# Reordering the last 90 microseconds of a fused cross-attention and expert-scaled feed-forward kernel

## What is computed

```python
def xattn(hs, ctx, mask, bias, ln_w, w_q, w_k, w_v, w_out):     # 32 heads of 128
    q, k, v = rmsnorm(hs, ln_w) @ w_q.T, ctx @ w_k.T, ctx @ w_v.T
    p = softmax(where(mask, q @ k.T + bias, -inf)); p = where(mask, p, 0)
    return hs + (p @ v) @ w_out.T

def ffn(x, weight, bias, gate_w, in_scale, out_scale):          # 8 experts, soft routing
    routing = softmax(x @ gate_w.T)
    return (x * (routing @ in_scale)) @ sign(weight).T * (routing @ out_scale) + bias

x = x + xattn(layernorm(x), ...)
x = x + ffn(layernorm(x), ...)
```

## Time and profile before

| what | us |
| --- | --- |
| median of 3 runs | 860.38 (859.5 to 860.78) |
| the profiled execution | 857.39 |
| its span, first to last instruction | 855.6 |
| PE / DVE / ACT / POOL busy | 840.8 / 630.6 / 390.4 / 301.8 |
| mean granted PE clock | 0.990 |

### The profile page before, as it was taken

The page is one execution under the profiler, slowest core; times in us unless marked ns, Lnnn a source line. Parts: engine busy times, 40 slices in busy tenths (PEclk is TensorE's granted clock), DMA queues, the critical chain, the costliest instruction groups (busy, mean ns, idle before and its releaser), DMA issues.

```text
span 855.6 us, 12845 instructions
## 1 busy us (share of the span) xinstructions
PE 840.8 (98%) x4348; PEld 705.3 (82%) x4348; DVE 630.6 (74%) x1011; ACT 390.4 (46%) x1005; POOL 301.8 (35%) x279
## 2 busy tenths in 40 slices
PE   9999999999999999999999999999999999999897
PEld 8878888888888877888888888888888888888775
DVE  5777846878775886867777777777787777789755
ACT  5633412432432444545554455455445545556642
POOL 2103211022020144534644544554354455423236
PEclk9999999999999999999999999999999999999969
DMA  8354464673453768314214412431442143150002
GB/s 278 127 194 170 158 218 135 208 241 123 136 173 106 233 197 285 123 53 151 105 53 154 151 67 91 152 111 52 149 152 88 69 153 112 47 209 7 1 0 100
DMA packets 60576, 114.07 MB, mean 133 GB/s; under 512 B 5192, under 2 KB 38600, under 8 KB 55264
## 3 DMA queue, kind: packets, MB, share of 16 engines
q1 hardware_dynamic: 60512, 113.25, 38.8%
HBM read 77.58 MB, written 35.65 MB: 132 GB/s over the span
## 4 chain that ended last, share of the span: by engine, by line
PE 87%; DVE 7%; issue 2%; ACT 2%; DMA 1%; POOL 0%; DVEq 0%; POOLq 0%; ACTq 0%; SPq 0%
PE out L1241 10%; PE out L1243 10%; PE out L1242 10%; PE proj L1241 8%; PE proj L1243 8%; PE proj L1242 8%; PE s L1313 6%; PE o L1332 6%; PE s L1243 3%; PE s L1241 3%; PE s L1242 3%; PE t L1321 3%; PE t L1360 1%; PE proj L1399 1%; PE s L1289 1%
## 5 line engine op out<-in xcount | busy, mean ns | idle before, releaser
L848 ACT ACTIVATE probs<-probs,neg_max 128x128 f32<-128x128 f32 x256 | 99.7, 391 | 137.3 <-DVE neg_max L1099 137.2
L697 POOL TENSOR_TENSOR w_stage<-w_stage 128x256 f32<-128x256 f32 x30 | 25.0, 833 | 309.1 <-DMA w_stage<-in_wk 132.7
L709 POOL TENSOR_TENSOR w_lo<-w_stage,w_hi 128x512 fp32r<-128x512 f32 (+1 forms) x52 | 59.2, 1149 | 144.8 <-ACT w_hi L786 144.8
L1131 DVE TENSOR_TENSOR acc<-out,acc 128x512 f32<-128x512 f32 x112 | 76.2, 687 | 36.5 <-PE out L1243 35.8
L1241 PE MATMUL out<-wo_hi,o_hi 128*128 128x512 f32 x224 | 95.1, 425 | 0.6 <-DVE acc L1131 0.6
L1241 PE MATMUL proj<-x_hi,w_hi 128*128 128x512 f32 x210 | 88.5, 422 | 0.2 <-DVE ring L958 0.2
L1243 PE MATMUL out<-wo_lo,o_hi 128*128 128x512 f32 x224 | 88.2, 394 | 0.0
L1242 PE MATMUL out<-wo_hi,o_lo 128*128 128x512 f32 x224 | 87.6, 391 | 0.0
L1243 PE MATMUL proj<-x_lo,w_hi 128*128 128x512 f32 x210 | 82.7, 394 | 0.0
L1242 PE MATMUL proj<-x_hi,w_lo 128*128 128x512 f32 x210 | 82.0, 391 | 0.0
L719 POOL TENSOR_TENSOR bias_mask<-bias_raw,mask_neg 128x512 f32<-128x512 f32 x64 | 76.0, 1199 | 14.5 <-DVE probs L1096 14.5
(11 more groups left out here) (318 smaller groups left out, 2153.3 us busy)
## 6 DMA issues: line engine op xcount, KB each, us to landing
k_spill<-ring SPq DMA_DIRECT2D x64, 256.0 KB, 2.7
v_spill<-ring SPq DMA_DIRECT2D x64, 256.0 KB, 2.2
w_stage<-in_wk SPq DMA_DIRECT2D x32, 256.0 KB, 3.4
big_stage<-in_wv SPq DMA_DIRECT2D x8, 1024.0 KB, 7.9
w_stage<-in_wq SPq DMA_DIRECT2D x32, 256.0 KB, 4.2
k_first<-k_spill SPq DMA_DIRECT2D x8, 1024.0 KB, 6.8
v_first<-v_spill SPq DMA_DIRECT2D x8, 1024.0 KB, 4.8
wo_raw<-in_wo SPq DMA_DIRECT2D x16, 512.0 KB, 3.3
```

Source lines behind the costliest of these rows:

```text
L709: pool.tensor_tensor(lo, staged(m, part), hi.bitcast(F32), ALU.subtract).then_inc(g_wlo, 1)
L848: last = act.activation(probs[:, j % 2, b, :], probs[:, j % 2, b, :], ACT.Exp, bias=neg_max[:, col:col + 1], accum_out=row_sum[:, col:col ...
L1131: dve.tensor_tensor(acc[:, b, :], out_bank[n % 2][:], acc[:, b, :], ALU.add).then_inc(v_acc, 1)
```

## The change

- The output products of the last two pairs, b and c, of one tile go into the same bank: c adds to what b left there. Tiles 0 to 7 use `proj0, proj1, out0, out1, out0, out1, proj0, proj1`. DVE adds only once for both.
- The steps of the last eight units are set anew: `ST` and the adds are spread differently, and `b`'s last tiles, `TX 0` and `TX 1` stand inside the last slot.
- `SCALES` goes from slot j + 4 to j + 2, and its low part from DVE to POOL, between two `BM`.
- `TX` uses the two score banks for all tiles.
- Tiles 4 and 6 are normalised by DVE, 5 and 7 by ACT. ACT's square root has a step of its own, `ROOT`.
- POOL's bias additions are steps of their own, `BI`, and several of them stand much later.
- `M` is cut into two parts (chunks 0 and 1, chunks 2 and 3), and the order of the feed-forward steps is new: tiles 0 and 1 are routed and multiplied before tiles 4 to 7 are transposed.
- A new step `KEEP` issues six matmuls of 512 columns whose result nobody reads.

```diff
@@ schedule()
-    steps += swift(j + 2, outs(a, 7), outs(b, 0), [("SIGN", 2)])
+    steps += swift(j + 2, outs(a, 7), outs(b, 0), [("SIGN", 2), ("SCALES",)])
     steps += swift(j + 3, outs(b, 1), outs(b, 2), [("SIGN", 3)])
-    steps += swift(j + 4, outs(b, 3), outs(c, 0), [*outs(c, 1), ("SCALES",), *outs(c, 2)])
-    steps += swift(j + 5, [], [("ST", 0), ("ST", 1), ("ST", 2), *outs(c, 3)], [])
-    steps += swift(j + 6, [], [("ST", 3), ("LN2", 0), *outs(b, 4)], [("LS", 0)])
-    steps += swift(j + 7, outs(b, 5), [("NT", 0), ("NT", 1), *outs(b, 6)], [("NT", 2), ("NT", 3)])
-    steps += [*outs(b, 7), ("TX", 0), ("TX", 1), *outs(c, 4), ("ST", 4), ("TX", 2), ("TX", 3), *outs(c, 5), ("ST", 5), ("G", 0),
-              *outs(c, 6), ("ST", 6), ("ROUTE", 0), *outs(c, 7), ("ST", 7), ("RT", 0), ("RTC", 0), ("LN2", 1), ("G", 1), ("R", 0),
-              ("LS", 1), ("NT", 4), ("NT", 5), ("NT", 6), ("NT", 7), ("TX", 4), ("TX", 5), ("OS", 0), ("TX", 6), ("TX", 7), ("OS", 1),
-              ("ROUTE", 1), ("Y", 0), ("G", 2), ("YL", 0), ("RT", 1), ("RTC", 1), ("G", 3), ("ROUTE", 2), ("R", 1), ("M", 0), ("Y", 1),
-              ("RT", 2), ("RTC", 2), ("YL", 1), ("MP", 0), ("OS", 2), ("M", 1), ("ROUTE", 3), ("R", 2), ("Y", 2), ("MP", 1), ("OS", 3),
-              ("RT", 3), ("RTC", 3), ("YL", 2), ("M", 2), ("R", 3), ("Y", 3), ("MP", 2), ("OS", 4), ("M", 3), ("YL", 3), ("MP", 3),
-              ("M", 4), ("MP", 4), ("OS", 5), ("M", 5), ("MP", 5), ("OS", 6), ("M", 6), ("MP", 6), ("OS", 7), ("M", 7), ("MP", 7)]
+    steps += swift(j + 4, outs(b, 3), outs(c, 0), [*outs(c, 1), ("ST", 0)])
+    steps += swift(j + 5, [*outs(c, 2), ("ST", 1)], outs(c, 3), [])
+    steps += slot(j + 6, [("ST", 2), ("ST", 3)], [("LN2", 0), ("ROOT", 0), *outs(b, 4)], outs(b, 5), [("LS", 0)], copy_first=True)
+    steps += swift(j + 7, [], [("NT", 0), ("NT", 1), *outs(b, 6)], [*outs(b, 7), ("TX", 0), ("TX", 1), ("NT", 2), ("NT", 3)])
+    def large(i):
+        return [("M", i, 0), ("M", i, 1)]
+    steps += [*outs(c, 4), ("ST", 4), ("BI", 0), ("BI", 1), ("G", 0), ("ROUTE", 0), *outs(c, 5), ("ST", 5), ("BI", 2), ("BI", 3),
+              ("TX", 2), ("TX", 3), ("RT", 0), ("RTC", 0), *outs(c, 6), ("R", 0), ("Y", 0), ("ST", 6), ("YL", 0), ("G", 1), ("ROUTE", 1),
+              *outs(c, 7), ("ST", 7), ("LN2", 1), ("ROOT", 1), *large(0), ("RT", 1), ("RTC", 1), ("OS", 0), ("LS", 1),
+              ("NT", 4), ("NT", 5), ("R", 1), ("NT", 6), ("NT", 7), *large(1), ("Y", 1), ("YL", 1), ("OS", 1), ("MP", 0),
+              ("TX", 4), ("TX", 5), ("TX", 6), ("TX", 7), ("MP", 1), ("M", 2, 0), ("G", 2), ("ROUTE", 2), ("BI", 4), ("M", 2, 1), ("OS", 2),
+              ("M", 3, 0), ("RT", 2), ("RTC", 2), ("G", 3), ("R", 2), ("Y", 2), ("M", 3, 1), ("YL", 2), ("MP", 2), ("OS", 3), ("KEEP", 0),
+              ("OS", 4), *large(4), ("ROUTE", 3), ("RT", 3), ("RTC", 3), ("R", 3), ("Y", 3), ("MP", 3), ("BI", 5), ("OS", 5), *large(5),
+              ("YL", 3), ("MP", 4), ("BI", 6), ("OS", 6), *large(6), ("MP", 5), ("BI", 7), ("OS", 7), *large(7), ("MP", 6), ("MP", 7)]
@@ banks, and who normalises
+        def output_bank(p, b):
+            if p >= LAST - 1:
+                return (proj_bank + out_bank + out_bank + proj_bank)[b]
+            return out_bank[nth_out[p, b] % 2]
         def ffn_bank(i):
-            return proj_bank[i % 2] if i < HALF else s_bank[i % 2]
+            return s_bank[i % 2]
+        BY_DVE = (4, 6)
@@ POOL: bias_and_mask, scales_low (was DVE's)
+                if j == SCALES_AFTER:
+                    pool.wait_ge(g_scales, 1)
+            def scales_low():
+                low = slice(32, 32 + E)
+                pool.wait_ge(g_bm, SCALES_AFTER)
+                pool.wait_ge(a_scales, 1)
+                pool.tensor_tensor(scales_split[low], scales_raw[low], scales_split[low].bitcast(F32),
+                                   ALU.subtract).then_inc(g_scales, 1)
@@ DVE: add_out
+                if p == LAST - 1:
+                    return
@@ PE: output, ffn_product, keep_busy
+                to = output_bank(p, b) if p == LAST else take(output_bank(p, b))
+            def keep_busy(_):
+                to = take(s_bank[1])
+                for _ in range(KEEP_BUSY):
+                    last = pe.matmul(to[:], sign_w[:, 0, 0:P], sign_w[:, 0, :], start=True, stop=True)
+                last.then_inc(pe_kept, 1)
```

More of the change, by code:

```diff
@@ L27 @@
 WARM_UP = 48
+KEEP_BUSY = 6
 MASKED = 2.0 ** 100
@@ L310, in xattn_ffn @@
     nth_out = {step[1:]: n for step, n in count("OUT").items()}
+    added = [step[1:] for step in steps if step[0] == "OUT" and step[1] != LAST - 1]
+    nth_add = {step: n + 1 for n, step in enumerate(added)}
     nth_split = {step[1:]: n for step, n in count("WX").items()}
@@ L453, in output_tiles @@
             return wo_hi[:], wo_lo[:]
+        SCALES_AFTER = len([step for step in steps[:steps.index(("SCALES",))] if step[0] == "BM"])
+        def output_bank(p, b):
+            if p >= LAST - 1:
+                return (proj_bank + out_bank + out_bank + proj_bank)[b]
+            return out_bank[nth_out[p, b] % 2]
         def ffn_bank(i):
-            return proj_bank[i % 2] if i < HALF else s_bank[i % 2]
+            return s_bank[i % 2]
+        BY_DVE = (4, 6)
         in_scale_bank = [o_bank, out_bank[0]]
         def normal_done(i):
-            return (a_n, i + 1) if i < HALF else (v_n, i - HALF + 1)
+            if i in BY_DVE:
+                return v_n, BY_DVE.index(i) + 1
+            return a_n, [k for k in range(B) if k not in BY_DVE].index(i) + 1
         def walk(parts):
@@ L1122, in add_out @@
                     dve.wait_ge(v_res, 4)
[L1123 removed]
+                    dve.scalar_tensor_tensor(out=acc[:, b, :], in0=acc[:, b, :], scalar=res_scale[:, b:b + 1], in1=bank_tensor[:],
                                              op0=ALU.mult, op1=ALU.add).then_inc(v_acc, 1)
                     return
[L1126 removed]
+                dve.wait_ge(v_acc, nth_add[p - 1 if p < LAST else LAST - 2, b])
                 if p == 1:
[L1128 removed]
+                    dve.scalar_tensor_tensor(out=acc[:, b, :], in0=bank_tensor[:], scalar=res_shift[:, b:b + 1], in1=acc[:, b, :],
                                              op0=ALU.add, op1=ALU.add).then_inc(v_acc, 1)
                     return
[L1131 removed]
+                dve.tensor_tensor(acc[:, b, :], bank_tensor[:], acc[:, b, :], ALU.add).then_inc(v_acc, 1)
             def ffn_statistics(b):
[L1134 removed]
+                dve.wait_ge(v_acc, nth_add[LAST, b])
                 dve.bn_stats(stats[:, b, :], acc[:, b, :]).then_inc(v_stats, 1)
@@ L1148, in normal_tile @@
             def normal_tile(i):
-                if i < HALF:
+                if i not in BY_DVE:
                     return
@@ L1219, in _ @@
                   "PV": out_low, "OUT": add_out, "ST": ffn_statistics, "LN2": ffn_norms, "LS": normal_scales, "NT": normal_tile,
-                  "SCALES": scales_low, "G": logit_maxima, "ROUTE": route, "Y": scale_tiles, "YL": scaled_low, "MP": scale_product})
+                  "G": logit_maxima, "ROUTE": route, "Y": scale_tiles, "YL": scaled_low, "MP": scale_product})
         @block.tensor
@@ L1342, in output @@
                 pe.wait_ge(v_olo, max(unit_at[2 * p + k, b // HALF] for k in range(2)) + 1)
-                to = take(out_bank[n % 2])
+                to = output_bank(p, b) if p == LAST else take(output_bank(p, b))
                 three(to, [(both(attended, everything, k, toks), both(tiles, everything, k, everything))
-                           for k in range(2)], pe_out)
-                read_by(to, v_acc, n)
+                           for k in range(2)], pe_out, p != LAST)
+                if p != LAST - 1:
+                    read_by(to, v_acc, nth_add[p, b])
             def ffn_transpose(i):
@@ L1389, in routed_out_scale, with ffn_product @@
                 read_by(to, a_os, i + 1)
-            def ffn_product(i):
-                if i == 0:
+            def ffn_product(i, part):
+                if i == 0 and part == 0:
                     pe.wait_ge(a_sign, DC)
-                to = take(proj_bank[i % 2])
+                to = proj_bank[i % 2] if part else take(proj_bank[i % 2])
                 toks = slice(i * P, (i + 1) * P)
-                for c in range(DC):
-                    if c % 2 == 0:
-                        pe.wait_ge(*scaled_low_done(i // 2, c // 2))
-                    pe.matmul(to[:], scaled_hi[:, c, toks], sign_w[:, c, :], start=c == 0, stop=False)
-                    last = pe.matmul(to[:], scaled_lo[:, c, toks], sign_w[:, c, :], start=False, stop=c == DC - 1)
-                last.then_inc(pe_ffn, 1)
-                read_by(to, v_prod, i + 1)
+                pe.wait_ge(*scaled_low_done(i // 2, part))
+                for c in (2 * part, 2 * part + 1):
+                    pe.matmul(to[:], scaled_hi[:, c, toks], sign_w[:, c, :], start=c == 0, stop=False, skip_group_check=True)
```

(9 more changed lines are left out.)

32 lines of the change are left out of this document (12 added, 20 removed).

## The result

| | median us | executions |
| --- | --- | --- |
| before | 860.47 | 4 (859.5 to 860.78) |
| after | 855.47 | 4 (854.82 to 857.07) |

A forecast was written before the change was run, and what follows sets the result against it. PE's own work was taken as the bound, except in the last attention units, the routing waits and the low clock. The terms moved the span's end from 855.6 to 851.3, 4.3 us, rounded to 4.6: 860.4 to 855.8, range 852.8 to 859.3.

The forecast's parts named there:

- attention, to c's tile 4: Last attention units: c's tile 4 starts at about 801.1 instead of 802.04, 0.9 us gained, bounds 0 to 1.5.
- c's tile 4 to the end of `R 3`: From c's tile 4 to the end of pair 3's input scales: 35.9 us instead of 38.2, ending at 837.0.
- of it: new waits: Before R 3 ends: +1.4 at R 1, +0.9 at TX 6 and TX 7, +0.4 at R 3; +2.7 us together.
- wait ahead of product 5: At M 5, PE stands about 1.2 us until MP 3 on DVE empties its bank at 838.6.
- POOL's last eight: POOL's last eight instructions, sum 3 to sum 6, take 1.28 us each, 10.2 us, ending at 848.8.
- `R 3` to the span's end: From R 3's end at 837.0 to the last store ending the span at 851.3, with POOL, not PE, last.
- low clock gone: -8.3: Routing stretch: PE's half-speed clock from about 814.8 to 831.9 disappears, saving 8.3 us.
- the rival of a partial fall: Clock falls once more for 4 to 7 us, costing 2 to 3.5; time 857.8 to 859.3; chance 0.20.
- Both named places: Thin spots where the clock might fall: RT 1, OS 0, the 1.4 us wait, R 1; OS 1, four transposes, 0.9 us wait.
- marks of a wrong forecast: Prediction called wrong if the clock is low for more than 4 us, or the span ends on DVE's last sum.
- the bias additions lie bare behind `MP 3`: At the end, three POOL bias additions behind MP 3 are no longer hidden by POOL's idle time around 800 and 815.
- POOL's contention with unit 60's normalisation: Near 779, a BM on POOL delayed by the scales' low part slows DVE's normalisation by 0.6 us, at most 0.9.

The follow-up runs named there:

- bias additions early: Bias additions 5, 6 and 7 earlier in POOL's queue, against the kernel with MP 3 ahead of Y 3; 851.44 us, ratio to before 0.9913.
- the sum first: MP 3 (output of tile 3) moved ahead of Y 3 (scaling of pair 3), against after; 852.41 us, ratio to before 0.9919.
- the scales move: Expert scales split two slots later, low part still on POOL, against the kernel with MP 3 ahead of Y 3; 852.01 us, ratio to before 0.9914.
- three moves without `KEEP`: MP 3 ahead of Y 3, bias additions 5 to 7 earlier, scales later, and no KEEP matmuls, against after; 852.53 us, ratio to before 0.9928.

## Why the prediction was right, and where it was right by luck

The time (855.8 forecast, 855.47 measured) and its direction were right, and the mechanism in the large too: attention alone gives almost nothing, the clock gives most, part of it is given back by new waits, and POOL's queue takes part in the end. By its own terms, against the profile:

| term | forecast | measured |
| --- | --- | --- |
| attention, to c's tile 4 | -0.9 | -1.4 (32.3 to 30.9 from unit 58's transpose) |
| c's tile 4 to the end of `R 3` | 35.9 | 36.2 (802.15 to about 838.3) |
| of it: clock | -8.3 | -6.6 (3.4 us still low, costing 1.7) |
| of it: new waits | +2.7 | +1.1 (0.3, 0.3 and 0.5) |
| wait ahead of product 5 | 1.2 | 1.5 |
| POOL's last eight | 10.2 | 10.3 |
| `R 3` to the span's end | 14.3 | 15.5 |

With the measured clock and waits the sum of the stretch to `R 3` gives 36.0 instead of 35.9, and 36.2 was measured. Counted from unit 58's transpose, the span of this execution is 3.3 us shorter than that of before, where the sum had 4.3.

**The clock.** The step "low clock gone: -8.3" was too large. It fell twice for 3.4 us, which is what the rival of a partial fall said (4 to 7 us). But neither place was one of the two named there: it fell beside c's tile 7, after the router products of pair 1, and at product 5. Both named places kept full clock, the stretch of the transposes of tiles 4 to 7 with its wait (821.2 to 823.5) too. Nor did the time of that rival come (857.8 to 859.3): the first fall cost 1.7 us, but the new waits were 1.6 us shorter than forecast, and the second fall lay beside POOL's queue. The text had made both a low clock of more than 4 us and an end on DVE's last sum into marks of a wrong forecast, and both were there. The number stood because errors cancelled. One argument of that rival was misread besides: the prediction has a run of transposes bring the clock up, as their rate goes from 7 to 12 in a microsecond, but the granted clock in both of the earlier trace rows is 1.00, so no row shows that the clock rose there.

**The new waits.** 2.7 us had been drawn up, 1.4 of them at `R 1` for ACT's copy behind its root. In after that wait is nothing, since the low clock at 813 made PE itself late. In the execution without KEEP, where the clock stayed up there, the two waits ahead of an input scale add up to 1.3 us, 0.8 of it at `R 1`. So the wait and the low clock are two prices for the same stretch, and an execution pays mostly the one or the other. The forecast had taken 2.7 us of waits and no low clock up to `R 3`; measured were 1.1 of waits and 1.7 for the clock, 2.8 together. That the two sums agree is luck.

**`KEEP`.** It was priced at 1.6 us, all of it on the path. The run without it shows a wait of 0.74 us in its place, so its net price is 0.8. It is also not sure to hold the clock: in the profiled execution with the bias additions early the clock fell within it.

**The end.** In before, the stretch behind `R 3` took 15.3 us with 4.5 us more of PE's work in it. So 4.7 us of what had been moved ahead of `R 3` was given back here; the forecast had 3.5. That the bias additions lie bare behind `MP 3` was right, and so was the wait ahead of product 5. POOL's last sum ended at 850.63; DVE's came 0.5 us later, because it contends with POOL for 1.54 instead of 0.69 us. The contention had been priced for attention and for POOL's sums, and forgotten for DVE's last sum. Of the 1.2 us by which the end was longer than forecast, that is 0.5, `MP 3` 0.3 (1.9 us behind `R 3`, not 1.6), and the rest lies in POOL's queue and the store. Putting the sum first and the bias additions early won 3.3 us of this end back (0.9951 to 0.9913). The second fall of the clock, which starts at the end of the very wait that was forecast, lay mostly beside POOL's queue: `M 7` ended at 848.9, and POOL had the last bias addition done only at 849.4.

**Attention.** The stretch gained 1.4 us, not 0.9, inside the bounds given. The 0.6 us of POOL's contention with unit 60's normalisation was right in kind and nearly in size: 1.62 us instead of 0.69, and 0.5 us back when the scales move.

**The base.** The sum was made on a profiled execution 3 us under its median. The low clock of before varies between executions by some 9 us of length, and that execution was at the short end. A sum on the median would have had to put the low clock at about 20 us and its price at 10. That the difference of two profiled executions is only 1.8 us, and that of the medians 5.0, would follow from these 1.7 us of price and the 1.5 us of the unchanged part.

What stays open: why the clock falls at 812 in one execution and not in the next with the same instructions ahead of it. No kernel here settles it. The profiled executions show only a pattern: where it did not fall near 812 (without `KEEP`, bias early, three moves without `KEEP`), it fell between 829 and 832, behind the router products and input scales of the next pairs.

## What to carry to other kernels

Where PE goes from large products to routing, transposes and other small work, read the granted clock in windows of 2 us, not in the slices of the page: a fall costs half its length where PE is the bound, and next to nothing beside another engine's queue. Here the new order of the feed-forward took the low clock from 17.1 to 6.8 us, worth some 5 us, and removed 3.2 us of old waits for 1.1 us of new ones up to `R 3`; the new order of the attention part alone gave nothing that the time could show. The stretch behind `R 3` gave 4.7 us back. After such a move walk each engine's queue once more from the last bound step on: here one DVE instruction behind two others, and three POOL instructions put where nothing hides them, together with the scales' place held back another 4 us (0.9951 to 0.9904). And compare kernels by the mean granted clock of each execution beside its time; it explained differences of 5 us between executions of one program, though not all of them.

## What the runs showed of the hardware that was not expected

- The clock fell at 813 in after although PE had waited no longer than 0.34 us in the 20 us ahead of it. What preceded it was small work: eight transposes, two more, four matmuls of 256 columns and 16 of 8, with one output tile between.
- ACT's table load does not wait for what its activation waits for: in after it starts at 813.80 and takes 1.28 us, and the root itself runs at 816.79, when its input is there.
- POOL takes as long over 8 partitions as over 128 (2.39 and 2.38 us for 1024 columns).
